# Mixture-of-experts block with attention on one core: opening reordered, weight splits moved one expert ahead

## What is computed

```python
xn = layernorm(x)                                        # 4 x 256 tokens, width 512
out = x + attention(xn) + ffn(xn)
# attention: 32 heads of 16 over 8 key/value groups, causal, softmax(q k / 4) v, then @ Wo + bo
# ffn, for each token:
scores = sigmoid(xn @ gate_w.T) + bias                   # 16 experts
topk_w, topk_idx = top_k(scores, 4); topk_w /= sum(topk_w)
out = sum over the chosen experts e of w_e * (silu(xn @ Wg[e].T) * (xn @ Wu[e].T)) @ Wd[e].T
out += silu(xn @ Sg.T) * (xn @ Su.T) @ Sd.T              # the shared expert, on every token
```

## Time and profile before

| | us |
|---|---|
| median of 3 runs (lowest, highest) | 566.04 (565.2, 567.9) |
| profiled execution, its time | 569.64 |
| profiled execution, its span | 567.9 |
| PE busy | 468.4 (82%) |
| DVE busy | 365.0 (64%) |
| POOL busy | 268.3 (47%) |
| ACT busy | 263.5 (46%) |

### The profile page before, as it was taken

How to read it: one execution, slowest core, us unless ns; L and a number is a source line. 1 busy time by engine, 2 the same in 40 slices (tenths; PEclk the granted TensorE clock), 3 DMA queues, 4 the chain that set the end, 5 groups by cost and what they waited for, 6 DMA issues and landing times.

```text
span 567.9 us, 9993 instructions
## 1 busy us (share of the span) xinstructions
PE 468.4 (82%) x2968; PEld 344.9 (61%) x2968; DVE 365.0 (64%) x606; ACT 263.5 (46%) x386; POOL 268.3 (47%) x234
## 2 busy tenths in 40 slices
PE   0995789968989997789878878997978899889880
PEld 0964578846667775367656655765656557667650
DVE  7377874676567957375779871787775546766510
ACT  2531212216555655165668642655736335645610
POOL 2002593304764652267546863573757336364510
PEclk9997999987998998899999899998989999889976
DMA  7804963336666557465687883668655534334222
GB/s 285 329 28 111 226 231 100 107 118 214 158 130 152 113 104 212 142 157 96 141 236 190 277 162 60 154 139 205 175 104 107 95 56 83 68 54 81 38 38 37
DMA packets 32060, 78.23 MB, mean 138 GB/s; under 512 B 4288, under 2 KB 11200, under 8 KB 28800
## 3 DMA queue, kind: packets, MB, share of 16 engines
q0 software_dynamic: 11936, 27.53, 26.8%
q1 hardware_dynamic: 17808, 43.96, 23.5%
q10 hardware_dynamic: 2256, 6.03, 5.0%
HBM read 54.04 MB, written 23.33 MB: 136 GB/s over the span
## 4 chain that ended last, share of the span: by engine, by line
PE 45%; DVE 15%; issue 8%; DMA 8%; ACT 8%; ACTq 6%; POOL 5%; SPq 2%; DVEq 1%; POOLq 1%
PE psum L1093 24%; PE psum L1221 5%; DMA q_parts<-stage 3%; ACT wsplit L573 3%; DVE negm L906 3%; PE psum L1187 2%; PE psum L1203 2%; POOL xn L446 2%; PE psum L1058 2%; ACTq L266 2%; PE psum L1115 2%; PE psum L1042 2%; POOL out L457 1%; PE psum L1103 1%; ACTq L264 1%
## 5 line engine op out<-in xcount | busy, mean ns | idle before, releaser
L1093 PE MATMUL psum<-wsplit,xgT 128*128 (+1 forms) x660 | 175.0, 416 | 0.2
L1093 PEld LDWEIGHTS psum<-wsplit,xgT 128*128 128x128 f32 x660 | 125.8, 197 | 30.3 <-issue 2.7
L457 POOL DMA_INDIRECT out<-ysb,tab x48 | 88.6, 1845 | 105.1 <-ACT ysb L606 84.2
L1093 PE MATMUL psum<-wsplit,zT 128*128 (+1 forms) x336 | 95.3, 420 | 29.0 <-DVE zT L898 29.0
L1093 PEld LDWEIGHTS psum<-wsplit,zT 128*128 128x128 f32 x336 | 61.6, 193 | 48.9 <-issue 37.6
L948 DVE TENSOR_TENSOR xgT<-psum,xgT 128x512 fp32r<-128x512 f32 x47 | 32.3, 688 | 65.4 <-ACT xgT L569 65.3
L437 POOL DMA_INDIRECT xg<-xn_rows,tab x47 | 51.9, 1104 | 29.6 <-PE psum L1231 20.0
L648 ACT ACTIVATE xn<-psum 128x1536 f32<-128x1536 f32 x32 | 46.5, 1453 | 40.6 <-PE psum L1189 40.6
L975 DVE TENSOR_TENSOR plo<-xn,phi 128x1536 f16<-128x1536 f32 x32 | 63.5, 1984 | 1.0
L446 POOL TENSOR_SCALAR_AFFINE_SELECT xn<-xn 128x512 f32<-128x512 f32 x64 | 55.3, 1060 | 7.9 <-ACT xn L648 7.8
L462 POOL TENSOR_TENSOR wsplit<-wraw,wsplit (+1 forms) x16 | 39.1, 2446 | 41.1 <-ACT wsplit L573 41.1
(11 more groups left out here) (180 smaller groups left out, 655.9 us busy)
## 6 DMA issues: line engine op xcount, KB each, us to landing
wraw<-wexp SPq DMA_DIRECT2D x17, 1024.0 KB, 6.1
wraw<-wexp SPq DMA_DIRECT2D x17, 512.0 KB, 4.6
q_parts<-stage SPq DMA_DIRECT2D x16, 192.0 KB
q_pack<-q_parts ACTq DMA_DIRECT2D x6, 384.0 KB, 4.6
xn<-x SPq DMA_DIRECT2D x4, 512.0 KB, 5.2
xn_rows<-xn SPq DMA_DIRECT2D x8, 256.0 KB, 7.6
ctxs<-x SPq DMA_DIRECT2D x8, 256.0 KB, 3.2
out<-ysb SPq DMA_DIRECT2D x8, 256.0 KB, 3.2
```

What stands on the lines that cost most here:

```text
L457: nc.gpsimd.indirect_dma_start(out=out, out_offset=rows_of(s), in_=ysb[:, par, :], in_offset=None, compute_op=ALU.add).then_inc(y_out[par] ...
L1093: last = MM(dst, lhs(a, k), split_weights(place, w, c), start=m == 0, stop=m == len(products) - 1)
```

## The change

- **PE in the opening.** The ranks follow on three projection units instead of four; in the loop over n, the projection of unit 4 + n comes after the shared expert's gate and up product; unit 4 uses bank 0, so that the first wait is for unit 0's remainder. Row maxima's first steps stand at n = 1, 2, 4, 6 in place of 1, 3, 5, 7. The transpose of the maxima and the first slot's rows are moved ahead.
- **DVE in the opening.** Remainders and splits stand one place earlier in the routing; three operations over tokens x choices x experts become four operations of one choice each (`of_choice`), used twice; `columns` is eight operations of one token tile each, with one scalar a row, for each of two tables, in place of one operation each; its four calls and `slot_experts` are spread over n = 0 to 3. `gated(0)` is moved ahead into the routing.
- **Values.** ACT makes the high parts, POOL the low parts.
- **Shared and first expert.** The shared expert's weights are split into place 1, so expert 0's can be split at n = 5 to 7.
- **Slots.** Gate and up weights of expert e are split in the first slot of expert e-1, behind all of that slot's other work on DVE and behind `high16` on ACT; down weights in the slot after. The place is worked out from the number. x and z parts no longer stand inside a branch.
- **Banks.** Gated values are transposed into bank 3; PE waits for `y_sb` ahead of `down`. The transposed maxima go to the bank of `weighted`, with a wait for `csum_done` ahead of the transpose and one for `nmT_sb` ahead of the batch's last `weighted`.

```diff
+MAXIMA_AT = {1: 0, 2: 1, 4: 2, 6: 3}
+SHARED = 1
...
-            return min(u, 3)
+            return min(u, 3) if u != EARLY else 0
...
+        ZB, NM = 3, PV
...
+                        s = SPS * b + j
+                        number = first_of(s - 1) if 1 < s < NSLOT else None
+                        if s < NSLOT:
+                            down_low_of(s, number)
...
+            pool.wait_ge(table_ps, 2)
+            value_rest(0)
+            down_low(0, 1)
+            pool.wait_ge(v_rest, 1)
+            value_rest(1)
             gather(2, 0, 1)
-            down_low(0, 1)
...
-                if t in (2, 4):
-                    xs_high_part(t // 2 - 1)
-                if t == 6:
-                    ws_high_part(0)
+                if t in (2, 3):
+                    xs_high_part(t - 2)
+                if t in (5, 7):
+                    ws_high_part(t // 2 - 2)
...
+            def gate_up_high(s, number):
+
+                if s == 0:
+                    weights_high(1, 2, HALVES[0], 0)
+                    weights_high(1, 2, HALVES[1], 0)
+                else:
+                    with act.If(number > 0):
+                        place = bass.ds((number + 1) % 2, 1)
+                        weights_high(place, number, HALVES[0], 0)
+                        weights_high(place, number, HALVES[1], 0)
+                    act.end_ifs()
+
+            def down_high(s, number):
+
+                if s == 1:
+                    weights_high(1, 2, PARTS[1], 1)
+                elif s > 1:
+                    with act.If(number > 0):
+                        weights_high(bass.ds((number + 1) % 2, 1), number, PARTS[1], 1)
+                    act.end_ifs()
...
+            for n in range(NT):
+                if n:
+                    z_high(n - 1, (n - 1) % 2, XT)
+                tanh(n, n % 2)
+                if n + 2 < NT:
+                    xs_high_part(n + 2)
+                if EARLY + n < UNITS:
+                    high_part(EARLY + n)
+                    middle_part(EARLY + n)
+                if n == 4:
+                    value_part(0)
+                if n == 5:
+                    weights_high(0, 1, HALVES[0], 0)
+                    weights_high(0, 1, HALVES[1], 0)
+                if n == 6:
+                    weights_high(0, 1, PARTS[1], 1)
+                    value_part(1)
+                if n == 7:
+                    minus_maxima(0, 0)
+            z_high(NT - 1, 1, ZB)
             x_high(0, 0)
+            value_part(2)
             act.wait_ge(slots_known, 1)
...
-                        s = SPS * b + j
-                        slot_parts(s, 1 - j % 2, not (last and j + 1 >= SPS - 1))
+                        s, par = SPS * b + j, j % 2
+                        if s + 1 < NSLOT:
+                            x_high(s + 1, 1 - par)
+                        z_high(s + (U1 - 1), 1 - par)
                         if j == BESIDE[g][-1] and (g == 3 or g == 7 and not last):
                             minus_maxima(2 * b + (g // 4 + 1), 1 - g // 4)
-                        if not (last and j == SPS - 1):
-                            tanh(s + U1, j % 2)
+                        if s < NSLOT:
+                            tanh(s + U1, par)
+                        number = first_of(s) if 0 < s < NSLOT else None
                         if j == BESIDE[g][0]:
                             high16(b, g)
-                        if not (last and j == SPS - 1):
-                            down_high(s)
+                        if s < NSLOT:
+                            gate_up_high(s, number)
+                            down_high(s, before)
                         y_evac(b, j)
+                        before = number
...
+            ws_low_part(1)
...
+            remainder(0)
...
             ws_low_part(2)
+            remainder(1)
...
-            remainder(1)
+            remainder(2)
...
-            op(V.tensor_tensor(oh[:, 0], per_choice(rt[:, 12, :, :]),
-                               kcount[:, :].rearrange("p (a k c) -> p a k c", a=1, c=1).broadcast_to([P, NT, TOPK, NE]),
...
-            op(V.tensor_tensor(oh[:, 1], oh[:, 0], per_choice(chosen), ALU.mult))
-            op(V.tensor_tensor(oh[:, 2], oh[:, 1], per_choice(rt[:, 13, :, :]), ALU.mult))
+            def of_choice(out_, values):
+
+                for k in range(TOPK):
+                    own.did(V.scalar_tensor_tensor(out=out_[:, :, k, :], in0=rt[:, 12, :, :], scalar=float(k + 1), in1=values,
+                                                   op0=ALU.is_equal, op1=ALU.mult))
+                own.wait()
+
+            of_choice(oh[:, 2], rt[:, 13, :, :])
...
-            remainder(2)
...
-            op(V.tensor_tensor(oh[:, 3], oh[:, 1], per_choice(rt[:, 1, :, :]), ALU.mult))
+            op(V.tensor_tensor(rt[:, 2, :, :], rt[:, 1, :, :], chosen, ALU.mult))
+            gated(0, 0)
+            of_choice(oh[:, 3], rt[:, 2, :, :])
...
-                slots = siota[:, :].rearrange("p (a n) -> p a n", a=1).broadcast_to([P, NT, NCOL])
-                V.tensor_tensor(at_col[:, k], slots, row_col[:, 1, :, k:k + 1].broadcast_to([P, NT, NCOL]),
-                                ALU.is_equal).then_inc(cols_set, 1)
-                V.tensor_tensor(at_row[:, k], lane[:, :].rearrange("p (a n) -> p a n", a=1).broadcast_to([P, NT, P]),
-                                row_col[:, 0, :, k:k + 1].broadcast_to([P, NT, P]), ALU.is_equal).then_inc(rows_set, 1)
+                for t in range(NT):
+                    last = V.tensor_scalar(at_col[:, k, t, :], siota[:, :], row_col[:, 1, t, k:k + 1], None, ALU.is_equal)
+                last.then_inc(cols_set, 1)
+                for t in range(NT):
+                    last = V.tensor_scalar(at_row[:, k, t, :], lane[:, :], row_col[:, 0, t, k:k + 1], None, ALU.is_equal)
+                last.then_inc(rows_set, 1)
...
+                if n:
+                    z_low(n - 1, (n - 1) % 2, XT)
+                    gated(n, n % 2)
+                if n + 2 < NT:
+                    xs_low_part(n + 2)
+                if n < 3:
+                    columns(n)
                 if EARLY + n < UNITS:
                     remainder(EARLY + n)
-                if n:
-                    z_low(n - 1, (n - 1) % 2, XT)
-                gated(n, n % 2)
-                if n + 2 < NT:
-                    xs_low_part(n + 2)
+                if n in MAXIMA_AT:
+                    maxima(MAXIMA_AT[n], MAXIMA_AT[n])
                 if n:
                     shared_out(n - 1)
-                if n == 0:
+                if n == 2:
+                    columns(3)
+                if n == 3:
                     slot_experts()
-                if n < 2:
-                    columns(2 * n)
-                    columns(2 * n + 1)
                 if n == 4:
                     slot_tokens()
                 if n == 6:
                     slot_gates()
-                if n % 2:
-                    maxima(n // 2, n // 2)
-                if n == 6:
-                    split_value(0)
+                    gu_low(0, 1, 0)
                 if n == 7:
-                    split_value(1)
...
-            z_low(NT - 1, 1, XT)
+                    gu_low(0, 1, 1)
+            z_low(NT - 1, 1, ZB)
+            x_low(0, 0)
...
+            def first_of(s):
+
+                return dve.value_load(where[0:1, 2, s + 1:s + 2], min_val=0, max_val=NE)
+
+            def gate_up_low(s, number):
+
+                if s == 0:
+                    gu_low(1, 2, 0)
+                    gu_low(1, 2, 1)
+                else:
+                    with dve.If(number > 0):
+                        gu_low(bass.ds((number + 1) % 2, 1), number, 0)
+                        gu_low(bass.ds((number + 1) % 2, 1), number, 1)
+                    dve.end_ifs()
...
-                        slot_parts(s, 1 - j % 2, not (last and j + 1 >= SPS - 1))
-                        if not (last and j == SPS - 1):
+                        if s + 1 < NSLOT:
+                            x_low(s + 1, 1 - j % 2)
+                        z_low(s + (U1 - 1), 1 - j % 2)
+                        if s < NSLOT:
                             gated(s + U1, j % 2)
+                        number = first_of(s) if 0 < s < NSLOT else None
...
+                        if s < NSLOT:
+                            gate_up_low(s, number)
...
-            gu_low(0, 1, 0)
-            gu_low(0, 1, 1)
-            x_low(0, 0)
...
-            for u in range(EARLY):
+            for u in range(EARLY - 1):
...
+            project(EARLY - 1)
...
-                if EARLY + n < UNITS:
-                    pe.wait_ge(rem_done, EARLY + n)
-                    project(EARLY + n)
                 if n:
                     z_transpose(n - 1, (n - 1) % 2, XT)
                 pe.wait_ge(xs_low, n + 1)
-                gate_up(n % 2, 0)
-                if n % 2:
+                gate_up(n % 2, SHARED)
+                if EARLY + n < UNITS:
```

(21 more changed lines are left out.)

205 lines of the change are left out of this document (78 added, 127 removed).

## The result

| | kernel before | kernel after |
|---|---|---|
| median of 4 runs each | 565.62 us (563.98 to 567.9) | 595.28 us (591.47 to 598.57) |
| ratio to before, 95% interval | | 1.052 (1.044 to 1.060) |
| profiled execution | 569.6 us, span 567.9 | 591.47 us, span 589.7 |
| first scores of the slots | 133.15 us | 125.55 us |
| first scores to the last work of TensorE (PE) | 421 us | 450 us |

The account below looks back on a forecast made before the run. PE itself was taken to bound 80 to 121.5 us, with 53 us idle in the slots. 569.6 - 7.5 - 2.4 - 7 - 1.3 + 1 = 552.4, less 3.6 for the median: 548.8 us, range 537 to 560.

Parts of the forecast that it names:

- The step that failed: Slots: with DVE's split last, maxima are on time and the next slot's x_low and z_low are late; gain 7 us.
- 23 us for 30: Slots: PE idle time put down to the 15 splits, 23 us at the new place instead of 30 at the old.
- six of the second [kind], where PE's slot has DVE idle and the split is free: Slots: six of the 15 splits fall in slots of the second kind and were taken to cost nothing.
- stays as it is: Slots 18 to 22, the bunch of one-slot experts: no change was expected there.
- 43 to 46 of 413: Sign to look for in the slots: PE idle 43 to 46 us of 413.
- The slower one: Rival, slots: ACT's splits delay y_evac and the exponentials, 3.2 us in all 15; time 574 us, chance 0.05.
- y_sb: Slots: moving PE's wait for y_sb behind gate_up gives -1.3 us, bounds 0 and -5.
- csum: Slots: the new wait for csum_done at seven transposes costs 0 to 0.5 us each, +1 us in sum.
- The maxima's waits: Sign to look for in the slots: PE's waits for the maxima, 5.7 us, all but gone.
- The opening: Before the slots: -7.5 us up to the token table and -2.4 behind it, 9.9 in all; slots start about 123.3.
- -2.4 us: End of the opening, behind the token table: PE idle 4.9 us in place of 7.3, bounds 0 and -5.
- columns: Opening, DVE: 2.2 us a call, 8.8 against 9.6 in sum, so no change.

Follow-up runs that it names:

- experiment 6: Kernel after with ACT's gate/up copies moved behind tanh and DVE's split right behind gated, ahead of maxima and context: 596.22 us, ratio 1.049.
- experiment 2: Also called `ahead_but_early`: kernel after with the gate/up splits still one expert ahead, but between z_low and gated, ACT's copies likewise before tanh: 560.8 us, ratio 0.986.
- experiment 1: Kernel after with the slots' weight splits put back to the schedule of the kernel before, opening and banks kept: 563.93 us, ratio 0.991.
- experiment 5: Kernel after with only ACT's gate/up copies moved ahead of high16, DVE's split left at the slot's end: 600.37 us, ratio 1.056.
- experiment 8: Kernel of experiment 2 with one half of DVE's gate/up split put back at the slot's end: 579.12 us, ratio 1.017.
- experiment 4: Kernel before with only the new banks and their waits for y_sb, csum_done and nmT_sb: 570.86 us, ratio 1.004.
- experiment 9: Kernel of experiment 2 with each table's columns built by a single operation instead of eight: 563.23 us, ratio 0.989.
- experiment 10: Kernel of experiment 2 with the maxima's transpose moved behind gate_up and ACT's copy of it behind tanh: 563.16 us, ratio 0.987.

## Why the prediction was wrong

**The step that failed** is "With the split at the end, the maxima are on time, but 2.36 more of DVE still follow low16 ... What is late is x_low and z_low of the next slot". Two things are wrong with it.

First, the consumer of the moved work itself was left out. The step followed who waits for what stands behind the split, and never asked who waits for the split. Behind an expert with one slot, the next expert's split stands in the slot right ahead of its own first; PE's gate_up comes there 2 to 7 us before DVE is at the end of its row. Moving the order one expert ahead hid this in the reading: the split is one expert ahead, but an expert can be one slot. That is where the 31.5 us of waits stand; experiment 6 shows that taking them away there brings them back elsewhere.

Second, the new place was priced below the old one, 23 us for 30. The prediction read 1.94 us of waiting for the maxima behind the split and took that away for the move. The old place does cost something, as experiment 2's rows show, but the new one costs 35 to 37 us more (experiments 1 and 2). It computed the slot's load on DVE (6.3 + 2.4 us against PE's 7.4) as if it mattered only in sum. But DVE's idle time is not in one heap: part of it lies between z_low and gated, while PE is busy with the very products that tanh needs. The earlier trace rows show the split in that gap. DVE's waits for tanh over the slots were 24.3 us in the kernel before, 23.5 in `ahead_but_early` and 48.0 in the kernel after: the change left idle a stretch that the split had used, and put the split where PE waits for it. A part of the loss came with that: the splits' operations take 49.5 us of DVE for 40.6 in `ahead_but_early` (beside GpSimd, below), and PE's clock fell in the second batch.

**"six of the second [kind], where PE's slot has DVE idle and the split is free"**: this may hold. The third batch of the kernel after loses nothing against the kernel before, with four splits, two of them in slots of the second kind. But of the seven waits for the split 2.12 and 2.15 us stand behind splits in slots of the second kind. The prediction also counted 2.2 us for each of the four slots for which it had found 2.4, which matters little. It was the bunch of one-slot experts, of which the prediction said that it "stays as it is", that took most of the second batch's 28.7 us. PE idles 82 of 450 us in the slots, for the forecast 43 to 46 of 413.

**Rivals.** The slower one had the wrong engine: ACT's order (experiment 5 moves its copies and gains nothing), though its arithmetic, a price per split times 15 against what today's splits cost, was the right form. The range ended at 560 because no rival priced DVE's split at its full duration in all 15 slots *on top of* today's time: 15 x 2.36 = 35 us. That this comes so near to the measured 37 is in part luck, by the spread over the batches in experiment 8.

**y_sb** (-1.3): nothing, experiment 4. **csum** (+1): 5.1 us in seven places, 0.7 each, above the bound of 0.5.

**The maxima's waits** "all but gone": no. They went from 5.7 us in 3 places to 7.6 in 14. z_low's were 24.9 us, inside the 12 to 28 that the prediction gave.

**The opening.** Up to the token table the profile agrees with the forecast: packs at 47.19 (forecast 48.2), landing of store 4 at 71.38 (73), the table's products at 82.00 (81.7). But the last agreement is luck, of terms that cancel. The last `columns` call took 7 us for 1.9 in the forecast's chain (77.1 to 79), its start came 2.2 us earlier than forecast, and the 2.7 us for POOL behind it did not come: POOL works beside it. PE's wait was 5.28 us for some 3.

Behind the table the forecast had -2.4 us, and this term was mis-sized. PE idles 7.5 us between the table's products and the first scores, for 7.4 before and a forecast of 4.9 (whose own items, 1.3 for z_low, 0.9 for the last shared output and 2.0 for the table, add up to 4.2). Measured were 2.9 for z_low in two places, 2.86 for the reading of the table, and 1.73 ahead of the maxima's transpose, which waits for DVE's table and for which the forecast had nothing. So the first scores stand at 125.55 and not at 123.3.

Even this is the best of its kind. Nine of the kernels here have this opening, one of them with two small operations less; their first scores stand at 125.55 to 130.98, the middle one at 129.53, and only that of the kernel after inside the named window of 121 to 126. The two kernels with the old opening have them at 133.15 and 132.55. So by the profiles the opening gave between 1.6 and 7.6 us, for the forecast 9.9: that it gains is shown, how much is not.

The other term that was mis-sized is `columns`: 2.2 us a call. The calls took 2.7, 4.5, 4.0 and 7.1. The first and the last, in DVE's timeline (the second part of the last call runs beside POOL's own work on the tables):

```profile
50.67 1.32 DVE L878 TENSOR_SCALAR xg<-siota,xn 128x48 bf16<-128x48 f32 x8
51.90 1.39 DVE L881 TENSOR_SCALAR xn<-lane,xn 128x128 bf16<-128x128 bf16 x8
...
76.17 5.77 DVE L881 TENSOR_SCALAR xn<-lane,xn 128x128 bf16<-128x128 bf16 x8
```

The first call's 48-column operations start 0.15 us from one another (eight in 1.23 us, up to the next line), not the 0.10 that the earlier trace rows showed for two of another form. The first call's 2.7 us are nearer to the estimate of some 3 us a call from the Trainium skill, "VectorE: DVE Perf Modes", section "The TRN2 errata", which the prediction had set aside. It was right to name it and wrong to overrule it by one pair of rows of another kind. As time no gain from undoing it can be measured (experiment 9).

## What to carry to other kernels

Ask of an engine's idle time not only how much of it there is but when: of work that stands where the engine would wait for something anyway, only the part beyond that wait costs, and the same work two instructions later, on the chain that the next engine waits for, cost 2.5 us more for each 2.36 us here, on the mean. For every piece of work that moves, price its own consumer first and then those behind it, and take the tightest case of the data (here the expert with a single slot). If moving late work ahead of other late work only renames the wait, look at the length of the whole chain before its order.

## What the runs showed of the hardware

**VectorE beside GpSimd.** POOL's `down_low` ran from 316.98 to 319.87 us in the wait shown above:

```profile
316.98 2.89 POOL L469 TENSOR_TENSOR wsplit<-wraw,wsplit  x1 [7.85 <-ACT wsplit L594]
```

and DVE's two split operations from 317.58 to 322.08, 4.50 us instead of 2.36. The first of the two took 3.36 us and the second 1.21. The first ends at 320.9, 1.1 us behind POOL's end: as if it had waited for POOL and then run at its usual 1.22. That is what the Trainium skill states ("SBUF — State Buffer", section "Terms": the port pair that the two engines share is held for a whole instruction and the loser blocks; "GPSIMD Engine Reference", section "1. Specifications": it concerns VectorE's instructions with two inputs in SBUF, as this one). The trace agrees; no run here isolates it. Five of the 15 splits of the kernel after took 4.50 to 4.56 us for their two operations, two took 2.79 and the others 2.36, and all of the slower ones stand in slots of the first kind; in `ahead_but_early` one took 4.52 and one 3.04.

The `columns` look alike: eight operations of 0.17 us took 0.72 each while POOL ran operations of 0.8 back to back, where the single operation of experiment 9 took 1.22 us in all. These have one tile and a per-row scalar as inputs, so they are not of the kind with two inputs, and whether the same cause is at work is not shown.

**The clock in stretches with waits.** PE's busy time in the second batch, where five of the seven waits for the split fall, rose by 8 us with the same instructions, at a granted clock of 0.88 for 0.98; that comes on top of the waits. The opening's clock varied as well: between two of the kernels with the same opening (the kernel after and that of experiment 10), the stretch from 90 us to the first scores ran at a clock of 1.00 and of 0.86, and the first scores came at 125.5 (kernel after) and at 131.0:

```profile
90.00:125.50 35.50, 28.01 (x194) 22.46 (x192) 23.46 (x48) 12.31 (x21) 13.80 (x9) 1.00 0.41 120
...
90.00:131.00 41.00, 34.09 (x208) 27.06 (x207) 26.12 (x51) 12.98 (x22) 15.82 (x11) 0.86 0.40 118
```

The clock is not all of it, since PE had 14 products more left at 90 us in the second of them. One profile of this opening is thus good to some 5 us, which is why its worth is better read from the runs of experiments 1 and 4. What decides which clock an execution gets there stays open.
